# An Euler polynomial in L taken three powers at a time inside the gaps of a tridiagonalization

## The reference, cut to what matters

```python
def _L0_gnn_ref(x, adj_mx, alpha_train, w, d, fc_in_w, fc_in_b, vt):
    x0 = x
    h = einsum('bnd,ed->bne', x, fc_in_w) + fc_in_b
    alph = sigmoid(alpha_train)[:, None]
    w_eff = w * clip(d, 0, 1) @ w.T
    for _ in range(8):                       # dt = 1/8
        ax = einsum('nm,bmd->bnd', adj_mx, h)
        h = h + dt * (alph * 0.5 * (ax - h) + h @ w_eff - h + x0)
    return h

def _L1_gnn_ref(features, A, ...):
    L_norm = d_inv_sqrt[:, None] * (diag(deg) - A) * d_inv_sqrt[None, :]
    _, U = eigh(L_norm)                      # 512 x 512
    ...                                      # relu(U.T f W1 + b1) W2 + b2, times U
```

## The kernel before, in words

| r | pieces in pause 0 and pause 1 |
|---|---|
| 1 to 21 | two or four per reflection, in some none: table and first inputs, each waiting for the one before |
| 22 to 112 | 2 and 2 |
| 113 to 126 | none, or two: first group ends, second group's inputs |
| 127 to 205 | 2 and 2 |
| 206 to 218 | none, or two: as above |
| 219 to 297 | 2 and 2 |
| 298 to 311 | none, or two: as above |
| 312 to 383 | 2 and 2 |
| 384 to 398 | 1 and 1 |
| 399 to 401 | none, or one |
| 402 to 510 | none: each pause issues one matmul of `IDLE` columns (`keep_clock`, L656), here 384 |

## Time and profile before

### The profile page before, as it was taken

One profiled execution on the slowest core, in us unless ns is written; L12 is line 12 of the kernel. 1 busy time (PEld: TensorE's weight loads), 2 busy tenths in 40 slices (PEclk: granted clock), 3 DMA queues, 4 the chain that ended last, 5 costly groups with the idle time before them and its releaser, 6 DMA issues.

```text
span 4554.4 us, 72277 instructions
## 1 busy us (share of the span) xinstructions
PE 3184.7 (70%) x22012; PEld 2163.8 (48%) x22012; DVE 2974.5 (65%) x18157; ACT 1019.2 (22%) x3735; POOL 780.0 (17%) x3360
## 2 busy tenths in 40 slices
PE   2999998998999999999400100000549584999998
PEld 1788877886887788655200000000426332444433
DVE  6687877888888888688878899999321223003323
ACT  0222222222222322222100000000031213116532
POOL 1122222222222222233222211111000000000000
PEclk7699996997998898599655555555779796889998
DMA  2000000000000000000000000000000000000000
GB/s 93 2 2 2 2 2 2 2 2 2 2 2 2 2 2 2 1 2 2 1 0 1 0 0 0 0 0 0 0 0 0 19 0 0 0 0 0 0 0 37
DMA packets 3104, 21.16 MB, mean 5 GB/s; under 512 B 432, under 2 KB 560, under 8 KB 1072
## 3 DMA queue, kind: packets, MB, share of 16 engines
q1 hardware_dynamic: 2736, 16.85, 0.9%
HBM read 12.66 MB, written 4.19 MB: 4 GB/s over the span
## 4 chain that ended last, share of the span: by engine, by line
PE 54%; DVE 33%; issue 5%; ACT 4%; POOL 3%; DMA 0%; DVEq 0%; SPq 0%; POOLq 0%; ACTq 0%
PE ps L621 7%; PE ps L951 6%; PE ps L664 6%; DVE H L1794 5%; PE ps L656 3%; PE ps L668 2%; PE ps L958 2%; PE ps L615 2%; PE ps L673 2%; PE ps L676 2%; DVE H L1383 2%; PE ps L524 2%; PE ps L923 2%; ACT H L1138 2%; PE ps L910 2%
## 5 line engine op out<-in xcount | busy, mean ns | idle before, releaser
L664 PE MATMUL ps<-C 128*32 128x131 f32 (+39 forms) x10200 | 394.9, 288 | 3.0 <-DVE C L1613 3.0
L1012 POOL TENSOR_SCALAR step<-XYEG,PQ 128x8 f32<-128x8 f32 (+3 forms) x510 | 157.9, 310 | 1236.2 <-DVE PQ L1546 1236.2
L1219 ACT ACTIVATE sz<-C,PQ 128x4 f32<-128x4 f32 (+3 forms) x510 | 151.6, 297 | 762.6 <-POOL C L1013 762.5
L621 PE MATMUL ps<-WK,LT 128*128 128x256 f32 x1024 | 307.6, 415 | 0.0
L621 PE MATMUL ps<-C,LT 128*128 128x256 f32 x1024 | 296.4, 405 | 0.0
L951 PE MATMUL ps<-C,V 128*128 128x512 f32 (+1 forms) x504 | 287.5, 727 | 8.5 <-issue 7.5
L664 PEld LDWEIGHTS ps<-C 128*32 128x32 f32 x10200 | 265.6, 118 | 39.8 <-DVE C L1613 14.5
L673 PEld LDWEIGHTS ps<-dots,ones 128*128 128x128 f32 x1020 | 177.2, 211 | 223.2 <-DVE dots L1383 145.9
L1203 ACT ACTIVATE tsc<-tsc 128x1 f32<-128x1 f32 x510 | 103.4, 203 | 768.6 <-DVE tsc L1507 768.6
L1383 DVE CUSTOM_DVE_ANT_0 jq<-SO,ps,C 128x10 f32<-128x10 f32 (+14 forms) x1199 | 220.1, 228 | 74.0 <-PE ps L686 25.0
L673 PE MATMUL ps<-dots,ones 128*128 128x2 f32 x1020 | 203.8, 270 | 60.7 <-DVE dots L1383 56.4
(11 more groups left out here) (484 smaller groups left out, 7613.2 us busy)
## 6 DMA issues: line engine op xcount, KB each, us to landing
out_x<-X SPq DMA_DIRECT2D x4, 1024.0 KB, 3.9
X<-in_x SPq DMA_DIRECT2D x2, 1280.0 KB, 20.6
X<-in_x SPq DMA_DIRECT2D x1, 1536.0 KB, 17.0
eye<-in_eye SPq DMA_DIRECT2D x1, 1026.0 KB, 9.4
WK<-in_adj SPq DMA_DIRECT2D x1, 1024.0 KB, 4.8
adjT<-in_adjT SPq DMA_DIRECT2D x1, 1024.0 KB, 6.9
WK<-in_below SPq DMA_DIRECT2D x1, 1024.0 KB, 11.0
V<-in_wih SPq DMA_DIRECT2D x1, 1024.0 KB, 4.9
```

The lines of the kernel that those rows point to most:

```text
L621: m = mm(some, LT[:, mb, j * P:(j + 1) * P], state(k + 1)[:, 2 * half:2 * half + 2, mb, :], start=False, stop=(part == last), skip_group_c ...
L664: m = mm(ps[q * QUAD:(q + 1) * QUAD, 0, 0:c + n], SI[:, b, 0, 2 * j:2 * j + 1].broadcast_to([P, QUAD]), AS[:, b, q, k * QUAD:P + n], start ...
L1012: step(g_.tensor_scalar(step2[:, k:KB, :], this[:, :, 2:4], PQ[:, r % 2, 1:2], None, ALU.mult))
```

## The change

It takes three powers per application: with y0 = x0, y1 = L x0, y2 = L^2 x0, the polynomial is s2 = y0 G_6 + y1 G_7 + y2 G_8; s1 = L^3 s2 + y0 G_3 + y1 G_4 + y2 G_5; s0 = L^3 s1 + y0 G_0 + y1 G_1 + y2 G_2 + bias part. L turned, L^2 and L^3 are made once, in 12 tiles ahead of the groups.

```diff
-IDLE = (256, 256, 256, 384)
+IDLE = (256, 256, 384, 384)
-ROOM = ((2, 2), (2, 2), (2, 2), (1, 1))
+ROOM = ((2, 1), (2, 1), (2, 1), (1, 1))
...
-TILES = 8 + 4 * EULER
+POWERS = 3
+SETUP = 12
+TILES = 4 * POWERS + 4 * (EULER + 1) // POWERS
+ALL_TILES = SETUP + 4 * TILES
...
     if t < SETUP:
         return None, ("L", "L2", "L3")[t // 4], t % 4, t
...
         elif kind in ("y1", "y2"):
             parts = [free + [("input", 8 * g + 2 * j + 1)]] * (2 * KB)
         else:
             parts = [free + [("tile", base + 4 * y + 2 * half + 1)] for y in range(POWERS) for half in range(2)]
             if kind != "s2":
                 parts += tiles(t - j - 4)
             if kind == "s0":
                 parts += [[w]] * 2
         i, r = p.unit(("tile", t), [free + n for n in parts], i)
         if kind == "y2" and j == 3:
             first = r + 1
         if kind == "s0":
             p.pool[r + 1].append(t)
...
-        above = TT
+        LM, L2, L3 = QT, LE, TT
+        Y2 = [DO[:, 0, :], DO[:, 1, :], VV[:, 2, :], VV[:, 3, :]]
...
-                mm(ps[:, 3, 0:2], ones[:], dots[:], start=True, stop=True).then_inc(S["dots_ps"], 1)
+                mm(ps[:, 3, 0:2], minus, dots[:], start=True, stop=True).then_inc(S["dots_ps"], 1)
...
-            for b in range(KB):
-                step(g_.memset(QT[:, b, :], 0.0))
-                m = g_.tensor_copy(QT[:, b, b * P:(b + 1) * P], ident)
...
-            g_.tensor_scalar(above, below, -1.0, None, ALU.mult).then_inc(S["above_ready"], 1)
...
                 for t_ in PLAN.pool[r]:
                     add_into_x(t_)
+                if EULER_END < r <= EULER_END + KB:
+                    identity(r - EULER_END - 1)
...
+            def identity(b):
+                pool.wait_ge(S["eu_sb"], ALL_TILES)
+                step(g_.memset(QT[:, b, :], 0.0))
+                g_.tensor_copy(QT[:, b, b * P:(b + 1) * P], ident).then_inc(S["qt_zero"], 1)
...
+            go(v.memset(minus, -1.0))
```

More of the change, by code:

```diff
@@ L174, in plan_gaps, with tiles @@
     i, first, out = start, 1, ("out", 0)
-    for t in range(4 * TILES):
-        g, k, j = tile_of(t)
+    def tiles(t0, n=KB):
+        return [[("tile", t0 + m)] for m in range(n) for _ in range(2)]
+    for t in range(ALL_TILES):
+        g, kind, j, place = tile_of(t)
         free = [("tile", t - BANKS)] if t >= BANKS else [out]
-        if k is None:
+        base = t - place
+        if kind == "L":
+            parts = [free] * 2
+        elif kind == "L2":
+            parts = tiles(0)
+        elif kind == "L3":
+            parts = tiles(4)
+        elif kind == "x0":
             if j == 0:
@@ L181, in plan_gaps @@
                     first = p.at(("input", 8 * g + h), first) + 1
-            i, _ = p.unit(("tile", t), [free + [("input", 8 * g + 2 * j + 1)]] * 2, i)
-        elif k == EULER:
-            i, _ = p.unit(("tile", t), [free + [("tile", t - 1 - j)]] * 2, i)
-        else:
[L186 to L190, removed]
+            parts = [free + [("input", 8 * g + 2 * j + 1)]] * 2
+        elif kind in ("y1", "y2"):
+            parts = [free + [("input", 8 * g + 2 * j + 1)]] * (2 * KB)
+        else:
+            parts = [free + [("tile", base + 4 * y + 2 * half + 1)] for y in range(POWERS) for half in range(2)]
+            if kind != "s2":
+                parts += tiles(t - j - 4)
+            if kind == "s0":
+                parts += [[w]] * 2
+        i, r = p.unit(("tile", t), [free + n for n in parts], i)
+        if kind == "y2" and j == 3:
+            first = r + 1
+        if kind == "s0":
+            p.pool[r + 1].append(t)
     assert max(p.seen.values()) < REFLECTIONS
@@ L592, in tile_part @@
             def tile_part(t, part):
-                g, k, j = tile_of(t)
-                bank = 4 + t % BANKS
+                g, kind, j, place = tile_of(t)
+                half, step_, base = part % 2, part // 2, t - place
+                bank = ps[:, 4 + t % BANKS, :]
+                some = bank[:, 2 * half * D:2 * (half + 1) * D]
                 if part == 0:
@@ L600, in tile_part @@
                         pe.wait_ge(S["table_sb"], EULER + 2)
[L601 to L619, removed]
-                        pe.wait_ge(S["eu_sb"], t - j - 4 + mb + 1)
[L621 to L626, removed]
+                if kind in ("L", "x0"):
+                    if kind == "x0":
+                        pe.wait_ge(S["x0_ready"], 8 * g + 2 * j + 2)
+                    for b in range(2 * half, 2 * half + 2):
+                        m = turn(bank[:, b * P:(b + 1) * P], LT[:, b, j * P:(j + 1) * P] if kind == "L" else B0[:, j, b, :])
+                    last = 1
+                elif kind in ("L2", "L3", "y1", "y2"):
+                    last = 2 * KB - 1
+                    if kind == "L2":
+                        pe.wait_ge(S["eu_sb"], step_ + 1)
+                    elif kind == "L3":
+                        pe.wait_ge(S["eu_sb"], KB + step_ + 1)
+                    elif kind == "y1":
+                        pe.wait_ge(S["x0_ready"], 8 * g + 2 * j + 2)
+                    turned = LM[:, step_, j * P:(j + 1) * P] if kind in ("L2", "L3") else B0[:, j, step_, :]
+                    m = mm(some, turned, (LT if kind in ("L2", "y1") else L2)[:, step_, 2 * half * D:2 * (half + 1) * D],
+                           start=(part == 0), stop=(part == last), skip_group_check=True)
+                else:
+                    stage = int(kind[1])
+                    last = 2 * POWERS - 1 + (2 * KB if stage < 2 else 0) + (2 if stage == 0 else 0)
+                    if step_ < POWERS:
+                        pe.wait_ge(S["eu_sb"], base + 4 * step_ + 2 * half + 2)
+                        n = POWERS * stage + step_
+                        for q in range(2 * half, 2 * half + 2):
+                            m = mm(bank[:, q * D:(q + 1) * D], power(step_, q)[:, j * P:(j + 1) * P],
+                                   W["fcT"] if n == EULER else G[:, n, :], start=(part == 0 and q == 0), stop=(part == last and q == 3),
+                                   skip_group_check=True)
+                    elif step_ < POWERS + KB and stage < 2:
+                        mb = step_ - POWERS
+                        pe.wait_ge(S["eu_sb"], t - j - 4 + mb + 1)
+                        m = mm(some, L3[:, mb, j * P:(j + 1) * P], state("s%d" % (stage + 1), mb)[:, 2 * half:2 * half + 2, :],
+                               start=False, stop=(part == last), skip_group_check=True)
+                    else:
+                        pe.wait_ge(S["w_tile_sb"], EULER + 1)
+                        m = mm(some, ident, w_of[EULER % 2][:, j, :].unsqueeze(1).broadcast_to([P, 2, D]),
+                               start=False, stop=(part == last), skip_group_check=True)
@@ L746, in vectors_update @@
                 else:
-                    pe.wait_ge(S["qt_zero"], 1)
+                    pe.wait_ge(S["qt_zero"], KB)
                 if lv < TOP:
```

53 lines of the change are left out of this document (28 added, 25 removed).

## The result

The changed kernel took 4522.5 us (median of 11 runs, 4495.9 to 4544.5) against 4549.8 us for the kernel before (11 runs, 4541.9 to 4556.3): ratio 0.9938, interval 0.9915 to 0.9961. It is faster by 0.6%: the 70 us that were forecast came out as 27. Its runs spread over 49 us, those of the kernel before over 14, and the time of a run goes with its mean granted clock: 0.805 of 2.4 GHz in the fastest, 0.792 in the slowest. The profiled execution took 4522.5 us, 33.7 under the one before.

What follows compares the result with a forecast made beforehand. It took half of the possible gain to be 1.2 GHz in place of 2.4, plus DVE's waits for PE at k = 0; terms summed to -70, giving 4483 us for the median, range 4430 to 4545.

Steps and rivals of the forecast that it cites:

- up to the first L1507: Setup: POOL's L997 goes, -3.4 us; the new memset on DVE costs 0.1 to 0.2.
- turnovers: Group changes at k = 0 to 2: inputs booked 30 reflections ahead, so the three stretches keep their pieces: -51 us.
- additions: POOL's additions into x hold DVE, +1.05 us each; eleven lie in full-clock stretches that had none; net +5 us.
- the gap at 328: Reflections 328 and 329 have no pieces or idle matmuls; clock falls until the panel update of r = 336: +13 us.
- identity: Four times on POOL, 0.52 and 0.29 us, in POOL's idle time; may hold DVE: 2 us taken.
- r = 384 to 415: Last group's end becomes idle reflections: -45 us, if they are reached at full clock.
- I take 25 such reflections beyond those of 330 to 335: +40: Half-clock reflections under three pieces at k = 2, +1.6 us each; bounds 0 and 200.
- rival A: Clock holds under three pieces everywhere but at 328 to 335: 4443 us, chance 0.2.
- the prediction's own signs of being wrong: Mean clock below 0.9 for r = 256 to 320, half clock at r = 384, or k = 0 reflections still 4.8 us.
- Rival C: After each addition at k = 1 and 2 the clock stays low up to the next panel update: 4533 us, chance 0.15.
- Rival B: Half clock becomes the normal state of k = 2, r = 256 to 383: 4651 us, chance 0.11.
- Rival D: At turnovers an input or eviction comes late, PE waits and the clock falls as before: 4534 us, chance 0.07.

Runs made afterwards that it cites:

- kernel with all places filled: Changed kernel plus filling matmuls at 16 additions, beside turned inputs, from r = 328 on, and extra columns at k = 2: 4436.0 us, ratio 0.9748.

## Why the prediction was wrong

Step by step, against the profiled executions:

| step | forecast | measured |
|---|---|---|
| up to the first L1507 | -3.2 | -2.8 (95.0 to 92.2) |
| r = 1 to 31 | -8 | -15.0 |
| r = 32 to 111 | -23 | -24.5 |
| r = 112 to 383: turnovers, additions, the gap at 328, identity, clock | -51 + 7 + 13 + 2 + 40, less 2 in 32 to 111 | +52.1 |
| r = 384 to 415 | -45 | -43.3 |
| r = 416 on | 0 | 0.0 |

(The 2 in that row is `identity`; the last 2 us are additions that lay in r = 32 to 111, so that this row's forecast is +11 and that of 32 to 111 becomes -25.)

The failed step is "I take 25 such reflections beyond those of 330 to 335: +40", that is 31 reflections at half clock. The mechanism stood there, and the price of one was right (72.00/14 = 5.14 us at half clock, forecast 5.1). The count was off: in the trace 63 of the 272 reflections from r = 112 to 383 start at half clock, a dozen of them in the stretch from 323 to 335. The kernel with all places filled has 4 of them and takes 89 us less there, where the forecast had 53 (40 and 13) for the clock; 89 us for 59 reflections are 1.5 each, forecast 1.6. These 36 us are most of the 41 by which the row is off. The terms beside the clock held in their sum: with all places filled the kernel takes 4436.0 us, and rival A, less its 13 us for r = 328 to 335, would be 4430. Two things made the count too low. I let only some of the additions bring the clock down; in this execution it was eight of the ten that met it at full clock. And I looked for falls at additions alone; the turned inputs, which the change moved out of the empty stretches into stretches of their own, bring it down too, and at k = 2 three pieces fail without any help. One of the prediction's own signs of being wrong was met: from r = 256 to 319 the mean clock was 0.86, under 0.9.

Rival C, low up to the next panel update after the additions, comes nearest: it said 4533, with chance 0.15. Behind r = 246 and 257 it happened so, and from the turned inputs of r = 194 on; behind r = 180, 186 and 191 the clock was back after 3 to 14 us, with three pieces and no panel update, so three pieces can raise it at k = 1. Rival A fell: the clock went down with PE idle for 1.23 us and no longer. The Trainium skill, "TensorE: Matmul & The Clock Gate", section "Why this matters for your kernels", asks that PE have no long idle gaps between bursts of matmuls; this kernel keeps to that with a longest gap of 1.3 us from r = 112 to 383, and the trace shows that it was not enough. Rival B did not come: the panel updates of k = 2 did raise the clock again. Rival D fell with the waits of PE, none for an input or an eviction, and with the stretch of r = 288 to 319 at full clock. The sign was right, and 4522.5 lies within the stated range; but the forecast's own range, 4460 to 4515, missed it. It lies in the upper part of that range, which was put there for rivals C and D and not for the forecast.

What stays open: whether turned blocks fail to hold the clock because a pause holds so little of them (0.42 us) or because they count for less; no run here separates the two. Nor does a run show why the same place loses the clock in one execution and not in another. `identity` was not left out by itself in any run, but the trace shows no price: beside its memset of 0.53 us at r = 330, DVE's L1624 took 0.22 us and L1431 0.23, as without it, and at r = 331 to 333 DVE was waiting for PE. The forecast had 2 us for it.

## What to carry to other kernels

When filler work on PE shares a chain with other engines, work out for each stretch not what PE has to do but whether it keeps its clock: taking work away can cost more than the work. Look at every operation that holds another engine (here POOL's 1.27 us addition) and at every stretch with only small pieces, and put an idle matmul there; in this kernel that alone was worth 87 us before the change (4466.8, and 4553.4 for the kernel before timed beside it) and 87 after it (4522.5 - 4436.0). It did not always hold: of the filled additions in three traces, three were still followed by a fall with nothing else beside them. And where runs of one kernel spread over 1% while those of its neighbour spread over 0.2%, look whether the granted clock differs from run to run: here it went from 0.792 to 0.805 in the changed kernel and from 0.828 to 0.831 in the filled one.

## What the runs showed of the hardware that I had not expected

The clock fell with PE busy 3.77 of 5.00 us:

```profile
919.50:924.50 5.00, 3.77 (x67) 3.28 (x56) 4.60 (x32) 0.89 (x5) 2.35 (x7) 1.00 0.00 0
924.50:930.00 5.50, 5.50 (x46) 4.65 (x38) 3.99 (x37) 0.89 (x5) 1.03 (x5) 0.50 0.00 1
```

(windows, all engines, first column behind the length is PE's busy time). And once low it can stay so although PE is shown busy all the time: 5.50 of 5.50 us right behind the fall, and 72.00 of 72.00 from 1283.0 to 1355.0 us, till a panel update put more matmuls close together. A panel update does not always do it: in the kernel before the clock stayed at half from 1784.2 to 1917.3 us, 133 us, through the panel update of r = 400, which had no idle matmul in it. At full clock, in the reflections from r = 416 on, PE is shown busy for 276.76 of 277.20 us. So the busy share on the page does not tell a PE that holds its clock from one that does not.
